# Window attention behind a depthwise convolution: attention blocks of one 8x8 patch and 32 channels, projection in quadrants, V transposed in the unit ring

## The chip, the core and the metric

The kernel runs on one core of one Trainium2 chip. The metric is the device time in microseconds. Below, PE is TensorE, DVE VectorE, ACT ScalarE, SP the engine that issues the loads and stores. All data is fp32.

## What is computed

x has the shape (4, 64, 128, 128). It is normalised in 32 groups of two channels and goes through a transposed channel attention, and x is added at the end:

```python
x = x + ref(gn(x))
qkv = einsum('bchw,oc->bohw', x, w_qkv) + b_qkv              # 192 channels
qkv = depthwise 3x3 convolution(qkv) + b_dw
# 8x8 windows, 4 heads of 16 channels; a window has 64 pixels
q, k, v = windows of qkv, each (windows, 4, 16, 64)
attn = softmax(einsum('nhcx,nhdx->nhcd', q, k) * temperature) # 16 x 16
out = einsum('nhcd,nhdx->nhcx', attn, v)
gate = gelu(einsum('nhcx,yx->nhcy', v, w_mlp) + b_mlp)        # exact gelu
out = einsum('bchw,oc->bohw', out * gate, w_proj) + b_proj
```

## The kernel before

Two images lie side by side in the 128 partitions (64 channels each), so there are two pairs of images. A pair is cut into 8 bands of 16 rows; a band of a pair is a chunk n, 16 in all. A chunk holds 64 windows (16 columns of windows, two window rows, two images). Work on chunk n + 1 up to q, k and v runs interleaved with the attention of chunk n.

The fore part of a chunk consists of units. 16 mix units (`mix_channels`, L674) put 10x10 patches through the 1x1 convolution: a unit is 4 matmuls, pixels on the output partitions. 6 depthwise units (`depthwise`, L709) multiply each channel's patch by a 103x64 matrix made from its taps: 32 matmuls a unit. One matmul of the source is two weight loads and two matmuls in the trace, a transpose one of each. Units share a ring of two PSUM buffers (`work`, two banks each in `unit_ps`). `units()` numbers all units in the order in which PE makes them; the parity of the number is the buffer. `take` makes PE wait until the unit two before it has been copied out, `wait_full` makes the copier wait for PE. ACT copies all mix units (z, L326) and most depthwise units (qkv, L326), DVE one a chunk (L417).

The attention of a chunk is four steps i of `BATCH` = 4 window groups, a = i % 4. A step is this chain:

- `score` (L747): per group, q times k with 64 pixels as contraction, for 64 columns of q (two windows of 32 channels) by 64 of k, into `score_ps`: 16 matmuls in 64x64 tiles. A 64x64 block also holds products between different windows and different heads, which are masked.
- DVE `scores_up`: adds the mask `other_head` (L511, 128x512), takes the maximum (L516), subtracts it (L518). ACT `exponent` (L341). DVE `divide`: sum (L532), reciprocal (L534), product (L536); `turn`: the 32x32 block transpose (L543) to `probs_t`.
- `turn_v` (L773): V of four groups is transposed on PE into `turn_ps`, one bank of `pair_ps`; ACT `v_up` (L347) copies it to `v_t`.
- `gates` (L763): V times w_mlp, 16 matmuls into `gate_ps`; DVE adds the bias (`gate_up`, L525), ACT does the gelu (L351), with table loads around it.
- `apply_probs` (L787): probabilities times V, 16 matmuls, into `pair_ps`; DVE `mix` multiplies by the gate (L503).
- `project` (L796): two matmuls of 128x128 by 256 columns, over a `proj` of 128x256 that is zero where a window half meets the other's channels, into `proj_ps`; DVE `residual` (L552) adds bias and x to `staged`, which SP stores by bands.

`pair_ps` holds three things in turn: `turn_ps` and the product of `apply_probs` use its first bank, `proj_ps` its second, so PE waits for `mixed_ready` of the step before ahead of `turn_v`, and for `out_ready` ahead of `apply_probs`.

The order of PE's work is written out by hand at the end of the PE block: score, some units (up to `cut[0]`), gates, project of the step before, turn_v, units up to `cut[1]`, gates, units up to `cut[2]`, apply_probs, the other units. Steps with a < 2 have 8 mix units each, a = 2 and a = 3 three depthwise units each. Gates are made in odd steps, two at once. ACT's and DVE's orders are written out in the same way; ACT is in step 0 and 1: two z copies, exp, v_t copy, six z copies; in step 2: v_t copy, exp, a qkv copy, gelus, a qkv copy; in step 3: exp, a qkv copy, v_t copy, gelu, qkv copy, gelu, qkv copy. The wait for both last depthwise units of a chunk stands before its first score (`qkv_of`).

## Time and profile before

| what | us |
|---|---|
| device time, three runs | 677.24, 678.43, 682.87 (median 678.43) |
| span of the profiled execution, first to last instruction | 680.0 |
| PE busy in it | 625.8 |
| DVE busy | 511.6 |
| ACT busy | 482.8 |

The profile gives no other time of its execution than the span; it is 1.6 us above the median of the runs. PE's busy time is made of modelled ends of matmuls that overlap, so starts are read rather than ends: how long a group takes is the distance from its first start to the first start of the next. PEld is the weight loads. "issue" is idle time for which the profile shows no releaser. Rows of the stretches view give busy time and, in brackets, the number of instructions that touch the stretch.

### The profile page before, as it was taken

The numbers are of one execution on the slowest core, as the hardware profiler recorded it, in microseconds if no ns is written. First come the engines' busy times: TensorE is split into PE (matmuls) and PEld (weight loads), VectorE is DVE, ScalarE is ACT, GpSimd is POOL, SyncE is SP. The second block draws the span as 40 slices with busy tenths as digits, with TensorE's granted clock in tenths as the row PEclk, the third lists the DMA queues.
The fourth block names the chain that finished last, engine by engine and source line by source line (L and its number), as shares of the span: only waits on it lengthen the run. The fifth ranks groups of instructions, "written<-read, shape, count | busy, mean of one in ns | idle before, by whom it ended". The sixth has DMA issues, their size and how long they took to land.

```text
span 680.0 us, 32438 instructions
## 1 busy us (share of the span) xinstructions
PE 625.8 (92%) x15044; PEld 549.1 (81%) x15044; DVE 511.6 (75%) x790; ACT 482.8 (71%) x631; POOL 0.3 (0%) x5
## 2 busy tenths in 40 slices
PE   3788799999999999999999999999999999999954
PEld 2687698888989898888989898888989798888843
DVE  4872688887888888786878676786868676876684
ACT  3652678787877778786877778786877778786722
...
PEclk9997899999999999999999999999999999999975
...
GB/s 363 263 217 72 33 50 166 110 86 208 33 232 49 234 59 149 66 102 93 8 191 5 195 4 142 60 94 106 29 173 4 198 3 152 44 50 80 4 82 44
DMA packets 29240, 72.28 MB, mean 106 GB/s; under 512 B 9801, under 2 KB 16329, under 8 KB 24233
## 3 DMA queue, kind: packets, MB, share of 16 engines
...
q8 instruction: 118, 1.93, 1.2%
...
q14 instruction: 16, 0.13, 0.1%
HBM read 53.44 MB, written 16.78 MB: 103 GB/s over the span
## 4 chain that ended last, share of the span: by engine, by line
PE 87%; ACT 5%; DVE 3%; issue 2%; DMA 1%; ACTq 0%; DVEq 0%
PE unit_ps L709 28%; PE unit_ps L674 26%; PE rest_ps L796 10%; PE rest_ps L787 6%; PE rest_ps L763 6%; PE rest_ps L747 6%; PE rest_ps L773 4%; ACT z L326 2%; DMA patches<-in_hot 1%; ACT dw L326 1%; PE rest_ps L643 1%; PE rest_ps L674 1%; PE unit_ps L636 0%; DVE scores L511 0%; DVE scores L536 0%
## 5 line engine op out<-in xcount | busy, mean ns | idle before, releaser
L326 ACT ACTIVATE z<-unit_ps 100x768 f32<-100x768 f32 x244 | 184.9, 808 | 60.1 <-PE unit_ps L674 60.1
L674 PE MATMUL unit_ps<-consts,patches 64*100 64x192 f32 x1984 | 195.0, 336 | 8.6 <-ACT z L326 6.6
L709 PE MATMUL unit_ps<-z,dw 103*64 103x64 f32 (+2 forms) x6144 | 194.3, 224 | 3.0 <-issue 1.7
L709 PEld LDWEIGHTS unit_ps<-z,dw 103*64 103x64 f32 (+2 forms) x6144 | 185.5, 139 | 10.7 <-issue 8.6
L674 PEld LDWEIGHTS unit_ps<-consts,patches 64*100 64x100 f32 x1984 | 153.6, 164 | 25.8 <-ACT z L326 11.2
L326 ACT ACTIVATE qkv<-unit_ps 128x1024 f32<-128x1024 f32 x78 | 79.1, 1014 | 31.5 <-PE unit_ps L709 31.4
L511 DVE TENSOR_TENSOR scores<-rest_ps,consts 128x512 f32<-128x512 f32 x64 | 44.1, 689 | 51.6 <-PE rest_ps L747 51.6
L503 DVE TENSOR_TENSOR gate<-rest_ps,gate 128x512 f32<-128x512 f32 x64 | 44.1, 689 | 47.5 <-PE rest_ps L787 44.6
L796 PE MATMUL rest_ps<-gate,consts 128*128 128x256 f32 x256 | 75.1, 417 | 1.1 <-DVE gate L503 1.0
L347 ACT ACTIVATE v_t<-rest_ps 128x512 f32<-128x512 f32 x64 | 38.2, 597 | 40.5 <-PE rest_ps L773 38.9
L341 ACT ACTIVATE scores<-scores 128x512 f32<-128x512 f32 x64 | 40.4, 631 | 33.2 <-DVE scores L518 31.6
L787 PE MATMUL rest_ps<-v_t,probs_t 64*64 64x64 f32 x2048 | 45.5, 228 | 10.5 <-DVE probs_t L543 10.1
L525 DVE TENSOR_TENSOR gate<-rest_ps,consts 128x512 f32<-128x512 f32 x64 | 44.0, 687 | 14.4 <-PE rest_ps L763 14.0
L796 PEld LDWEIGHTS rest_ps<-gate,consts 128*128 128x128 f32 x256 | 44.9, 195 | 11.9 <-issue 3.5
L747 PE MATMUL rest_ps<-qkv 64*64 64x64 f32 x2048 | 45.4, 227 | 9.0 <-issue 9.0
L787 PEld LDWEIGHTS rest_ps<-v_t,probs_t 64*64 64x64 f32 x2048 | 36.7, 137 | 20.9 <-issue 18.8
L747 PEld LDWEIGHTS rest_ps<-qkv 64*64 64x64 f32 x2048 | 37.9, 138 | 18.1 <-issue 18.1
L552 DVE SCALAR_TENSOR_TENSOR staged<-rest_ps,consts,staged 128x512 f32<-128x512 f32 x64 | 46.7, 729 | 7.5 <-PE rest_ps L796 7.5
L543 DVE STREAM_TRANSPOSE probs_t<-scores 128x512 f32<-128x512 f32 x64 | 45.5, 712 | 2.2
L763 PE MATMUL rest_ps<-consts,qkv 64*64 64x64 f32 x2048 | 45.6, 228 | 1.6 <-DVE scores L511 1.6
L763 PEld LDWEIGHTS rest_ps<-consts,qkv 64*64 64x64 f32 x2048 | 36.7, 138 | 12.3 <-issue 8.2
L518 DVE TENSOR_TENSOR scores<-scores,neg_max 128x512 f32<-128x512 f32 x64 | 44.3, 692 | 2.2
...
## 6 DMA issues: line engine op xcount, KB each, us to landing
...
```

Source lines behind the costliest of these rows:

```text
L326: return nc.scalar.activation(to, of, ACT.Copy)
L503: nc.vector.tensor_tensor(held, pair_ps[:, :, 0:BATCH * HW], held, ALU.mult).then_inc(mixed_ready, 1)
L511: nc.vector.tensor_tensor(scores[:].rearrange("p (h g) d -> p h g d", h=2), score_ps[:, :, 0:BATCH * C].rearrange("p h (g d) -> p h g d", ...
L518: nc.vector.tensor_tensor(scores[:], scores[:], neg_max[:].unsqueeze(2).to_broadcast([P, WIDE, C]), ALU.add).then_inc(shifted, 1)
L543: nc.vector.transpose(probs_t[:].rearrange("p w d -> p (w d)"), scores[:].rearrange("p w d -> p (w d)")).then_inc(probs_t_ready, 1)
L552: nc.vector.scalar_tensor_tensor(to, proj_ps.rearrange("p (r c) -> p r c", r=BAND), b_proj, to, op0=ALU.add, op1=ALU.add).then_inc(out_rea ...
L674: last = nc.tensor.matmul(to[0:NPATCH, t, b * QKV:(b + 1) * QKV], patches[image, b, g], w1[image], start=True, stop=True)
L709: last = nc.tensor.matmul(to[h * HW:(h + 1) * HW, m // 8, m % 8 * NW:(m % 8 + 1) * NW], dw[0:used, c, :], z[0:used, c, :], start=True, sto ...
L747: last = nc.tensor.matmul(score_ps[pair, h, g * C:(g + 1) * C], q[rows, pair], k[rows, pair], start=True, stop=True)
L763: last = nc.tensor.matmul(gate_ps[side(b, h), b, g * HW:(g + 1) * HW], windows(j, g)[rows, 2, b * C:(b + 1) * C], mlp[rows], start=True, s ...
L787: last = nc.tensor.matmul(pair_ps[side(b, h), b, g * HW:(g + 1) * HW], probs_t[rows, h * BATCH + g, :], v_t[rows, at], start=True, stop=True)
L796: last = nc.tensor.matmul(proj_ps[:, b * 4 * HW:(b + 1) * 4 * HW], proj[:, b * P:(b + 1) * P], gate[:, i % GATES, b].rearrange("p g (r c) ...
```

## The change

A block of the attention becomes one 8x8 patch of one image and 32 channels (two heads), in tiles of 32 columns. `score`, `gates` and `apply_probs` issue 32 matmuls each instead of 16. Scores, softmax and `probs_t` have 256 columns instead of 512 (`HALF` = 32 instead of `C` = 64 channels). `project` issues 4 matmuls, each of 64x64 weights by 256 columns, in the four quadrants, and its weights have no zeros. The result of `apply_probs` lies in the first halves of the two banks of `pair_ps`, that of `project` in the second halves. V is transposed into a buffer of the unit ring: ("turn", i) is a unit with a number of its own, so each step has one unit more, `turn_v` waits for its buffer instead of for `mixed_ready`, and `v_up` frees it. Constants loaded at the start are smaller by 160 columns.

```diff
@@ -64,7 +66,8 @@
     order = [("mean", 0), ("var", 0)]
     order += [("dw", 0, v) for v in range(3 * HALF // SPLIT)]
     for i in range(STEPS):
-        order += fillers(i)
+        fill, at = fillers(i), cuts(i)[0]
+        order += fill[:at] + [("turn", i)] + fill[at:]
     return {name: at for at, name in enumerate(order)}
 
 
@@ -84,6 +87,12 @@
     return fill
 
 
+def cuts(i):
+
+    a = i % BATCHES
+    return (2, 4, 6) if a < 2 else (0, 1, 3) if a == 2 else (1, 2, 3)
+
+
 def gates_in(i):
 
...
         T = sb("T", [P, BAND + 2, W + 2])
         patches = sb("patches", [P, 2, COLS, NPATCH])
         seen = sb("seen", [P, 2, STAT_ROWS, W])
-        scores = sb("scores", [P, WIDE, C])
-        probs_t = sb("probs_t", [P, WIDE, C])
+        scores = sb("scores", [P, WIDE, HALF])
+        probs_t = sb("probs_t", [P, WIDE, HALF])
         v_t = sb("v_t", [P, BATCH * P])
         gate = sb("gate", [P, GATES, 2, BATCH, HW])
...
@@ -131,7 +140,7 @@
         zeros = sb("zeros", [P, 2 * (BAND + 2)])
         norm = sb("norm", [P, PAIRS, 2])
 
-        sizes = (P, P, HW, 2 * P, QKV, C, HW, 1)
+        sizes = (P, P, HW, 2 * C, QKV, HALF, HW, 1)
         consts = sb("consts", [P, sum(sizes)])
         at = [sum(sizes[:n]) for n in range(len(sizes) + 1)]
         ident, group_mean, mlp, proj, w1, other_head, b_mlp, b_proj = (
@@ -148,9 +157,9 @@
         work = [unit_ps[:, 0:2], unit_ps[:, 2:4]]
         quarter = [half[:, 2 * m:2 * m + 2] for half in banks for m in range(2)]
         pair_ps = rest_ps[:, 0:2]
-        turn_ps, proj_ps = pair_ps[:, 0], pair_ps[:, 1]
-        score_ps = rest_ps[:, 2:4]
-        gate_ps = score_ps[:, :, BATCH * C:]
+        mix_ps, proj_ps = pair_ps[:, :, 0:BATCH * HW], pair_ps[:, :, BATCH * HW:]
+        gate_ps = rest_ps[:, 2:4, BATCH * HW:]
+        score_ps = rest_ps[:, 2:4, 0:BATCH * HALF]
 
         x_in = [sem(f"x_in{n}") for n in range(BANDS)]
...
@@ -234,7 +241,7 @@
 
             unit = ("dw", n, v)
             if n > 1:
-                engine.wait_ge(v_t_done, (n - 1) * BATCHES)
+                wait_full(engine, ("turn", (n - 1) * BATCHES - 1))
             wait_full(engine, unit)
             kind, at = kind_of(v)
             copy(qkv[:, n % 2, kind, :, at:at + SPLIT],
@@ -341,10 +348,11 @@
                 nc.scalar.activation(scores[:], scores[:], ACT.Exp).then_inc(exp_ready, 1)
 
             def v_up(i):
-                act.wait_ge(v_t_done, i + 1)
+                unit = ("turn", i)
                 if i:
                     act.wait_ge(mix_done, i)
-                nc.scalar.activation(v_t[:], turn_ps, ACT.Copy).then_inc(v_t_ready, 1)
+                wait_full(act, unit)
+                copy(v_t[:], work[buffer(unit)][:, 0]).then_inc(free[buffer(unit)], 1)
 
             def gelu(j):
...
                 held = gate[:, i % GATES].rearrange("p b g y -> p b (g y)")
-                nc.vector.tensor_tensor(held, pair_ps[:, :, 0:BATCH * HW], held, ALU.mult).then_inc(mixed_ready, 1)
+                nc.vector.tensor_tensor(held, mix_ps, held, ALU.mult).then_inc(mixed_ready, 1)
 
             def scores_up(i):
...
                 dve.wait_ge(scores_done, i + 1)
                 if i:
                     dve.wait_ge(probs_t_ready, i)
-                over = [P, 2, BATCH, C]
+                over = [P, 2, BATCH, HALF]
                 nc.vector.tensor_tensor(scores[:].rearrange("p (h g) d -> p h g d", h=2),
-                                        score_ps[:, :, 0:BATCH * C].rearrange("p h (g d) -> p h g d", d=C),
+                                        score_ps.rearrange("p h (g d) -> p h g d", d=HALF),
                                         other_head.unsqueeze(1).unsqueeze(1).to_broadcast(over),
                                         ALU.add).then_inc(masked, 1)
                 dve.wait_ge(masked, i + 1)
                 nc.vector.tensor_reduce(neg_max[:], scores[:], AX_X, ALU.max, negate=True).then_inc(max_ready, 1)
...
-                to = staged[:, n % 2, :, a * BATCH * WS:(a + 1) * BATCH * WS]
-                nc.vector.scalar_tensor_tensor(to, proj_ps.rearrange("p (r c) -> p r c", r=BAND),
+                to = staged[:, n % 2, :, a * BATCH * WS:(a + 1) * BATCH * WS].rearrange("p (b r) c -> p b r c", b=2)
+                nc.vector.scalar_tensor_tensor(to, proj_ps.rearrange("p b (r c) -> p b r c", r=WS),
                                                b_proj, to, op0=ALU.add, op1=ALU.add).then_inc(out_ready, 1)
 
...
@@ -730,8 +738,12 @@
                 at = 4 * (i % BATCHES * BATCH + g)
                 return qkv[:, i // BATCHES % 2, :, at:at + 4].rearrange("p k w c -> p k (w c)")
 
-            def side(b, h):
-                return slice((h ^ b) * HW, (h ^ b) * HW + HW)
+            def window(b, t):
+                return slice((2 * b + t) * HALF, (2 * b + t + 1) * HALF)
+
+            def place(b, t, h):
+                at = (2 * (t ^ b) + (h ^ b)) * HALF
+                return slice(at, at + HALF)
 
             def score(i):
 
@@ -740,12 +752,10 @@
                     pe.wait_ge(gate_biased, max(j for m in range(i) for j in gates_in(m)) + 1)
                 for g in range(BATCH):
                     q, k = windows(i, g)[:, 0], windows(i, g)[:, 1]
-                    for b in range(2):
-                        pair = slice(b * C, (b + 1) * C)
-                        for h in range(2):
-                            rows = slice(h * HW, (h + 1) * HW)
-                            last = nc.tensor.matmul(score_ps[pair, h, g * C:(g + 1) * C], q[rows, pair], k[rows, pair],
-                                                    start=True, stop=True)
+                    for b, t, h in product(range(2), repeat=3):
+                        rows = slice(h * HW, (h + 1) * HW)
+                        last = nc.tensor.matmul(score_ps[window(b, t), h, g * HALF:(g + 1) * HALF],
+                                                q[rows, window(b, t)], k[rows, window(b, t)], start=True, stop=True)
                 last.then_inc(scores_done, 1)
 
             def gates(j, i):
@@ -757,44 +767,42 @@
                     wait_free(pe, ("dw", j // BATCHES, 0))
                     wait_free(pe, ("dw", j // BATCHES, 1))
                 for g in range(BATCH):
-                    for b in range(2):
-                        for h in range(2):
-                            rows = slice(h * HW, (h + 1) * HW)
-                            last = nc.tensor.matmul(gate_ps[side(b, h), b, g * HW:(g + 1) * HW],
-                                                    windows(j, g)[rows, 2, b * C:(b + 1) * C], mlp[rows],
-                                                    start=True, stop=True)
+                    for b, t, h in product(range(2), repeat=3):
+                        rows = slice(h * HW, (h + 1) * HW)
+                        last = nc.tensor.matmul(gate_ps[place(b, t, h), b, g * HW:(g + 1) * HW],
+                                                windows(j, g)[rows, 2, window(b, t)], mlp[rows],
+                                                start=True, stop=True)
                 last.then_inc(gate_done, 1)
 
             def turn_v(i):
 
-                if i:
-                    pe.wait_ge(mixed_ready, i)
+                unit = ("turn", i)
+                to = take(unit)
                 for g in range(BATCH):
-                    last = nc.tensor.transpose(pair_ps[:, 0, g * P:(g + 1) * P], windows(i, g)[:, 2], ident)
-                last.then_inc(v_t_done, 1)
+                    last = nc.tensor.transpose(to[:, 0, g * P:(g + 1) * P], windows(i, g)[:, 2], ident)
+                last.then_inc(full[buffer(unit)], 1)
 
             def apply_probs(i):
 
-                pe.wait_ge(v_t_ready, i + 1)
+                wait_free(pe, ("turn", i))
                 pe.wait_ge(probs_t_ready, i + 1)
                 if i:
                     pe.wait_ge(out_ready, i)
                 for g in range(BATCH):
-                    for h in range(2):
+                    for h, b, t in product(range(2), repeat=3):
                         at = slice((2 * g + h) * HW, (2 * g + h + 1) * HW)
-                        for b in range(2):
-                            rows = slice(b * C, (b + 1) * C)
-                            last = nc.tensor.matmul(pair_ps[side(b, h), b, g * HW:(g + 1) * HW],
-                                                    probs_t[rows, h * BATCH + g, :], v_t[rows, at],
-                                                    start=True, stop=True)
+                        last = nc.tensor.matmul(mix_ps[place(b, t, h), b, g * HW:(g + 1) * HW],
+                                                probs_t[window(b, t), h * BATCH + g, :], v_t[window(b, t), at],
+                                                start=True, stop=True)
                 last.then_inc(mix_done, 1)
 
             def project(i):
 
                 pe.wait_ge(mixed_ready, i + 1)
-                for b in range(2):
-                    last = nc.tensor.matmul(proj_ps[:, b * 4 * HW:(b + 1) * 4 * HW], proj[:, b * P:(b + 1) * P],
-                                            gate[:, i % GATES, b].rearrange("p g (r c) -> p r g c", c=WS),
+                for b, t in product(range(2), repeat=2):
+                    rows = slice((t ^ b) * C, (t ^ b) * C + C)
+                    last = nc.tensor.matmul(proj_ps[t * C:(t + 1) * C, b], proj[rows, b * C:(b + 1) * C],
+                                            gate[rows, i % GATES, b].rearrange("p g (r c) -> p r g c", c=WS),
                                             start=True, stop=True)
                 last.then_inc(proj_done, 1)
 
@@ -815,7 +823,7 @@
             for i in range(STEPS):
                 units_now = fillers(i)
                 now = gates_in(i)
-                cut = (2, 4, 6) if i % BATCHES < 2 else (0, 1, 3) if i % BATCHES == 2 else (1, 2, 3)
+                cut = cuts(i)
                 if i % BATCHES == 0:
                     qkv_of(i // BATCHES)
...
     w_proj = np.asarray(L0_conv_w_proj)
-    proj = np.zeros((2, 2, HALF, 2, 2, C), f)
-    for b in range(2):
-        for h in range(2):
-            for t in range(2):
-                proj[h ^ b, t, :, b, t] = w_proj[:, h * HALF:(h + 1) * HALF].T
+    by_half = w_proj.T.reshape(2, HALF, C)
+    proj = np.stack([np.concatenate([by_half[b], by_half[1 - b]] * 2) for b in range(2)], 1)
     arrays = {
         "x": np.asarray(x),
```

PE in step 1 of a chunk (a = 1), from project to apply and the units behind it, before. `free0` and `free1` are the ring's buffers, `masked` and `gate_biased` DVE's passes:

```order
L796 MATMUL rest_ps<-gate,consts 128x256 [waits mixed_ready]
L796 MATMUL rest_ps<-gate,consts 128x256
L773 MATMUL rest_ps<-consts,qkv 128x128 [waits mixed_ready]
L773 MATMUL rest_ps<-consts,qkv 128x128 x3
L674 MATMUL unit_ps<-consts,patches 100x192 [waits free0]
L674 MATMUL unit_ps<-consts,patches 100x192 x3
L674 MATMUL unit_ps<-consts,patches 100x192 [waits free1]
L674 MATMUL unit_ps<-consts,patches 100x192 x3
L763 MATMUL rest_ps<-consts,qkv 64x64 [waits gate_biased,masked]
L763 MATMUL rest_ps<-consts,qkv 64x64 x15
L674 MATMUL unit_ps<-consts,patches 100x192 [waits free0]
L674 MATMUL unit_ps<-consts,patches 100x192 x3
L674 MATMUL unit_ps<-consts,patches 100x192 [waits free1]
L674 MATMUL unit_ps<-consts,patches 100x192 x3
```

and now:

```order
L804 MATMUL rest_ps<-gate,consts 64x256 [waits mixed_ready]
L804 MATMUL rest_ps<-gate,consts 64x256 x3
L782 MATMUL unit_ps<-consts,qkv 128x128 [waits free1]
L782 MATMUL unit_ps<-consts,qkv 128x128 x3
L682 MATMUL unit_ps<-consts,patches 100x192 [waits free0]
L682 MATMUL unit_ps<-consts,patches 100x192 x3
L682 MATMUL unit_ps<-consts,patches 100x192 [waits free1]
L682 MATMUL unit_ps<-consts,patches 100x192 x3
L772 MATMUL rest_ps<-consts,qkv 32x64 [waits gate_biased,masked]
L772 MATMUL rest_ps<-consts,qkv 32x64 x31
L682 MATMUL unit_ps<-consts,patches 100x192 [waits free0]
L682 MATMUL unit_ps<-consts,patches 100x192 x3
L682 MATMUL unit_ps<-consts,patches 100x192 [waits free1]
L682 MATMUL unit_ps<-consts,patches 100x192 x3
```

The transpose writes `unit_ps` and waits for a ring buffer, and the buffers of the units behind it alternate the other way round; project is 4 matmuls and gates 32.

PE from apply of step 2 through the first gates of step 3, before:

```order
L787 MATMUL rest_ps<-v_t,probs_t 64x64 [waits out_ready,probs_t_ready,v_t_ready]
L787 MATMUL rest_ps<-v_t,probs_t 64x64 x15
L747 MATMUL rest_ps<-qkv 64x64 [waits gate_biased,masked]
L747 MATMUL rest_ps<-qkv 64x64 x15
L709 MATMUL unit_ps<-z,dw 64x64 [waits free1]
L709 MATMUL unit_ps<-z,dw 64x64 x31
L763 MATMUL rest_ps<-consts,qkv 64x64 [waits free0,free1,gate_biased,masked]
L763 MATMUL rest_ps<-consts,qkv 64x64 x15
```

and now:

```order
L794 MATMUL rest_ps<-v_t,probs_t 32x64 [waits out_ready,probs_t_ready,free0]
L794 MATMUL rest_ps<-v_t,probs_t 32x64 x31
L757 MATMUL rest_ps<-qkv 32x32 [waits gate_biased,masked]
L757 MATMUL rest_ps<-qkv 32x32 x31
L717 MATMUL unit_ps<-z,dw 64x64 [waits free0]
L717 MATMUL unit_ps<-z,dw 64x64 x31
L772 MATMUL rest_ps<-consts,qkv 32x64 [waits free1,free0,gate_biased,masked]
L772 MATMUL rest_ps<-consts,qkv 32x64 x31
```

The order is the same; the matmuls of apply, score and gates are twice as many, those of the unit between them are not. In the same chunk, ACT's v_t copy reads `unit_ps` and waits for `full0` or `full1` instead of `v_t_done`.

## Rows read from the trace of the kernel before

**Rows 1.** The profile's page: busy shares, granted clock, instruction queue, chain.
```profile
PE 625.8 (92%) x15044; PEld 549.1 (81%) x15044; DVE 511.6 (75%) x790; ACT 482.8 (71%) x631; POOL 0.3 (0%) x5
...
PEclk9997899999999999999999999999999999999975
...
q8 instruction: 118, 1.93, 1.2%
...
PE 87%; ACT 5%; DVE 3%; issue 2%; DMA 1%; ACTq 0%; DVEq 0%
```

**Rows 2.** Stretches: length, busy PE, PEld, DVE, ACT, POOL; clock, DMA share, GB/s.
```profile
453.36:491.36 38.00, 37.14 (x928) 32.62 (x929) 28.52 (x44) 29.47 (x40) 0.00 (x0) 1.00 0.27 90
480.69:491.36 10.67, 10.06 (x341) 9.23 (x333) 8.49 (x14) 8.49 (x12) 0.00 (x0) 1.00 0.03 6
```

**Rows 3.** The chain that ended last, in that chunk: start us, us, what.
```profile
480.87 0.47 PE rest_ps L747 x32
...
490.75 0.61 issue
```

**Rows 4.** Timeline of PE: four first matmuls of a score, then step 0.
```profile
309.55 0.29 PE L747 MATMUL rest_ps<-qkv 64*64 64x64 f32 x4
...
453.36 0.69 PE L747 MATMUL rest_ps<-qkv 64*64 64x64 f32 x32 [0.60 <-issue]
453.98 1.55 PE L674 MATMUL unit_ps<-consts,patches 64*100 64x192 f32 x16
455.46 1.13 PE L796 MATMUL rest_ps<-gate,consts 128*128 128x256 f32 x4
456.43 0.60 PE L773 MATMUL rest_ps<-consts,qkv 128*128 128x128 f32 x4
```

**Rows 5.** Timeline of step 3 of the same chunk, PE and ACT.
```profile
481.27 2.08 PE L709 MATMUL unit_ps<-z,dw 103*64 103x64 f32 x64
...
483.28 0.69 PE L763 MATMUL rest_ps<-consts,qkv 64*64 64x64 f32 x32
483.71 0.63 ACT L341 ACTIVATE scores<-scores 128x512 f32<-128x512 f32 x1 [1.17 <-DVE scores L518]
...
484.25 1.01 ACT L326 ACTIVATE qkv<-unit_ps 128x1024 f32<-128x1024 f32 x1
```

**Rows 6.** Groups of instructions by line: busy us, mean ns, idle before them.
```profile
L511 DVE TENSOR_TENSOR scores<-rest_ps,consts 128x512 f32<-128x512 f32 x64 | 44.1, 689 | 51.6 <-PE rest_ps L747 51.6
...
L534 DVE RECIPROCAL inv_total<-total 128x8 f32<-128x8 f32 x64 | 13.0, 203 | 2.2
```

**Rows 7.** Stretch of the last four steps, columns as in rows 2.
```profile
643.73:676.60 32.87, 19.77 (x356) 15.55 (x356) 24.84 (x40) 10.01 (x15) 0.00 (x0) 0.70 0.23 58
```

**Rows 8.** Three places where PE stops: stretches, PE's timeline, instruction queue (55.5:56.8, 99.9:101).
```profile
51.96:58.11 6.15, 4.48 (x154) 4.34 (x149) 2.42 (x2) 1.03 (x1) 0.00 (x0) 1.00 0.57 174
98.70:102.31 3.61, 3.56 (x160) 3.41 (x153) 3.42 (x6) 2.14 (x4) 0.00 (x0) 1.00 0.28 77
249.92:253.49 3.57, 3.57 (x150) 3.44 (x148) 3.54 (x6) 3.02 (x5) 0.00 (x0) 1.00 0.17 37
...
58.12 0.39 PE L709 MATMUL unit_ps<-z,dw 106*64 106x64 f32 x6 [1.68 <-issue]
...
101.56 0.69 PE L763 MATMUL rest_ps<-consts,qkv 64*64 64x64 f32 x32
102.32 1.02 PE L796 MATMUL rest_ps<-gate,consts 128*128 128x256 f32 x4
...
633.27 2.45 PE L709 MATMUL unit_ps<-z,dw 106*64 106x64 f32 x64
...
q8 instruction: 1, 0.02, 5.7%
...
q8 instruction: 1, 0.02, 5.2%
```

**Rows 9.** Stretch after the first stop, columns as in rows 2.
```profile
59.60:73.20 13.60, 11.42 (x158) 9.84 (x152) 6.18 (x9) 4.52 (x6) 0.00 (x0) 0.50 0.00 1
```

13 lines of the change are left out of this document (6 added, 7 removed).

## The prediction

> **What bounds the kernel now.** I read the page's busy shares first: TensorE (PE) is busy 92% of the span, VectorE (DVE) 75%, ScalarE (ACT) 71% [rows 1]. The granted clock is full but for two places near the ends. The chain that ended last is 87% PE. Next the table of stretches for one chunk of four steps, 453.36 to 491.36 us: 38.00 us, PE busy 37.14 of it with 928 matmul instructions, ACT 29.5, DVE 28.5 [rows 2]. So PE sets the pace. The largest exception is before the next chunk's score: 0.6 us of "issue" [rows 3], at a place where the code waits for ACT's last qkv copy.
>
> The page counts 15044 matmuls and as many weight loads, and DMA queue 8 (kind instruction) brought 1.93 MB in 118 packets: 64 bytes an instruction, 16 KB a packet, so one packet is 256 PE instructions, or 128 load-and-matmul pairs [rows 1]. PE's program is streamed in. I come back to this, since the change makes that program longer.
>
> **The change, as PE's work.** One matmul of the source is two pairs in the trace (16 for 32).
>
> Score, gates and apply: 16 matmuls on 64x64 tiles become 32 on tiles of 32 columns, eight tiles side by side instead of four. Four tiles now do 32 pairs from one group's start to the next in 0.62 us [rows 4], of which some 0.15 us is the change of tile shape: without one, from apply to score, the chain has 0.47 [rows 3]. Eight tiles with the same 64 moving columns need the same eight rounds if they really run side by side, so 64 pairs in 0.62 us; score, with 32 columns, perhaps 0.02 less. The other bound is the densest issue that the rows show over a whole group, 32 pairs in those 0.47 us, or 14.6 ns a pair: by it 64 pairs take 0.94 + 0.15 = 1.09 us, 0.47 more in each of 12 groups, 5.6 us a chunk. I take 0.62, since four pairs are seen to start within 0.03 us [rows 4], so that the issue is not what spaces them.
>
> Project: 4 instructions of 256 columns now last 0.97 us [rows 4]. They become 8 in four quadrants, so two rounds of 0.22, a first weight load, and a change of shape that was not there (0.15): 0.60. The turn's first weight load then has no project to hide behind, 0.10. Net -0.27 a step; from below, if the quadrants ran one after the other, +0.9. The gates already run four such quadrants, with both row halves on one bank, in 0.62 us for 32 pairs, so I take -0.27. Apply to score, from step 2 to 3, gets a change of shape that it did not have, +0.15. PE alone: 4 x -0.27 - 0.08 + 0.15 = -1.0 us a chunk.
>
> **The ring.** The turn of V now takes a buffer of the unit ring, and the second mix after it waits for ACT's v_t copy (0.6 us). In step 0, counted from score's start, project starts at 2.06, the turn at 2.66, its copy at about 3.40, after exp, so the buffer is free at 4.0; that mix is due at 4.03. The mix after it keeps such wait for ACT as it has. In step 3 dw 4 needs the copy of dw 3, which ACT does after exp; before, exp began 3.0 us into the step [rows 4, 5]. Three DVE passes in front of it shrink by 0.25 each, so dw 3's copy ends near 3.9 and dw 4 is due at 4.5. I cost the ring at nothing; if the copies came late it is 0.3 to 0.6 in steps 0, 1 and 3, 1.5 a chunk.
>
> **DVE and ACT.** Seven DVE passes over 128x512 become 128x256: 0.69 to some 0.44 by the slope against the 128x8 reciprocal (0.20); exp goes from 0.63 to some 0.44, by the slope between 512 and the 1.01 of a 128x1024 copy [rows 6]. PE hides all of it in the chunks. It shows in the last four steps, which have no units to fill them: score, add, max, subtract, exp, sum, reciprocal, product, transpose, apply stand one behind the other, and DVE is the busiest engine there, 24.8 of 32.9 us [rows 7]. Seven times 0.25 is 1.75 us a step, 7 us; from both sides 3 (other waits come last) and 7; I take 6.
>
> **The instruction stream.** PE's pairs in a chunk go from 928 to 928 + 12 x 32 + 4 x 4 = 1328, so 10.4 packets in 37.0 us, one each 3.56 us. What does one cost? At 56.2 us PE stops for 1.9 us in the midst of a depthwise unit, where the code has no wait. A packet of queue 8 moves between 55.5 and 56.8, at 5.7% of 16 engines in 1.3 us, which is 1.19 us; PE goes on at 58.12, some 1.35 after its end. Two weaker stops look the same: L796 starts at 102.32, 0.76 after gates where 0.63 is usual, and 1.4 after the end of the packet that starts at 99.95 and takes 0.92; and in the unit at 633.27 64 pairs last 2.45 us where 2.08 is usual [rows 5, 8]. From counts of pairs: a packet is asked for when PE's queue enters the one before, some 18 pairs ahead of the array, so PE has some 146 pairs to run meanwhile. Before the stop at 102.3 these lasted 3.61 us; before the first one, with a load of T on the queues, 6.15. The densest such stretch that does not stop lasts 3.57 [rows 8]. So the stream's turnaround is about 3.5 us on quiet queues (1.0 to start, 1.1 to move, 1.35 to be used), and the kernel already touches it: the two weak stops lie where apply, score and a depthwise unit, 128 pairs in some 3.1 us, follow one another.
>
> After the change that seam has apply and score back to back, 128 pairs in 1.24 us. From that apply through step 3 to the next score: 588 pairs, 4.6 packets, that PE would do in 11.6 us (two applies and two scores 2.4, three depthwise units 6.0, two gates 1.2, project and turn 1.3, the wait for ACT 0.7). The three depthwise units of step 2 cover one packet, about four turnarounds remain, 4 x 3.5 = 14.0: +2.4 us. In step 1 gates, mix and apply are 128 pairs in 2.6 to 2.9: +0.3. Loads on the other queues stretch a turnaround as at 56 us (a T load is issued at each chunk's end); I put that at +1.0 a chunk. The waits for ACT go under these stops, -0.5. Sum +3.2; from both sides 0 (the chunks of now, which do not stop) and some 10, with four turnarounds of 6.15 instead of 3.5 there.
>
> The Trainium skill speaks against this term (Runtime: NRT & Kernel Launch, Instruction fetch mechanics): the fetch of 16 KB blocks is autonomous and hidden by the issue rate, and PE's instruction memory is given as 128 KiB. The trace agrees on the 16 KB; with that much in store (2048 instructions, by the page) the stop at 56.2 us would not be there. By the page the sum is rival A.
>
> **Sum.** Chunk: -1.0 + 3.2 = +2.2, times 15 = +33. Last four steps -6. The fill of the pipeline: 0. Span 680.0 + 27 = 707.0. The span of the profiled execution stands 1.6 above the median of the runs, 678.4, so 705 us.
>
> **Rivals.**
> A: the stream is hidden, as by the page, and PE's work counts alone: 678.4 - 15 x 1.0 - 6 = 657. For it: the chunk of 38.00 us has no such stop, PE being busy 37.14 of it [rows 2]. Against: the three stops, and 3.57 us as the densest stretch without one. If half of the stream's term comes (a second request under way, say), 680: no change.
> B: the tiles of 32 columns are not issued faster than 14.6 ns a pair. 5.6 us more PE work a chunk, which then hides most stops (1.0 left): -1.0 + 5.6 + 1.0, times 15, -6: 756. Against: four pairs start within 0.03 us [rows 4]. The Trainium skill (TensorE: Matmul & The Clock Gate, Wait — 56ns, not 53.3ns?) goes further: no less than about 25 ns between starts, however small the matmul. By it a group of 64 pairs would take 1.6 us; the rows have 14.6 ns, so it gets no chance.
> C: the stops pull the clock down. After the stop at 56.2 the granted clock is 0.50 from 59.6 to 73.2 [rows 9], at which PE's work takes about twice as long: some 5 us lost. With a stop that long in every other chunk, 7 x 5 on top: 742. It decides from stops of near 1.9 us; mine are 0.5 to 1.6, longer under a load.
>
> Chances: my forecast 0.50 (its own range 690 to 725), A 0.16, half of the stream's term 0.10, B 0.11, C 0.13. A measurement here tells about 1% from no change: faster by more 0.19, within 0.08, slower by more 0.73. The range takes A in and ends short of B: 655 to 750.
>
> **What would show it.** Right: queue 8 with about 168 packets and 2.75 MB; matmuls 21444; step 3 near 12 to 13 us instead of 10.67 and steps 0 to 2 shorter than or like before; PE idle that the waits put to "issue", at places in the midst of groups; score, gates and apply at 0.6 us where nothing stops them; project 0.60 to the turn's start; DVE's passes at 0.44. Wrong: chunks of 37 us without such gaps (A); groups of 1.1 us with PE busy throughout (B); a granted clock below 0.97 as a mean (C); waits for ACT's v_t copy before a mix, which would be the ring.

## The result and the profile after

| | us |
|---|---|
| before, median | 678.13 |
| after, median of four runs | 781.42 (777.75 to 785.61) |
| ratio, with 95% interval | 1.151 (1.146 to 1.157) |
| span of the profiled execution, after (before 680.0) | 783.8 |
| first score to the score of step 60 | 66.0 to 746.6 (before 66.7 to 643.7) |
| that score to the end | 37.2 (before 36.3) |

The change costs 103 us, where 27 were forecast. The profiled execution of after is the longest of its four runs (785.61), so what is read from it may be up to 4 us, or 0.3 a chunk, above the median. Practically all of it lies in the chunks: from the score of step 4 to that of step 60, 14 chunks, the mean chunk is 45.42 us instead of 38.15. Its four steps are 12.41, 11.30, 8.64 and 13.07 us (before 9.11, 9.95, 8.39 and 10.71).

The page of after, for [rows 1]:

```profile
PE 669.9 (85%) x21444; PEld 552.8 (71%) x21444; DVE 411.4 (52%) x790; ACT 475.0 (61%) x631; POOL 0.3 (0%) x5
...
PEclk9999999999997999989999999989989998999976
...
q8 instruction: 168, 2.75, 1.4%
...
PE 82%; issue 10%; ACT 5%; DVE 2%; DMA 1%; ACTq 0%; DVEq 0%
```

Counts are as forecast: 21444 matmuls, 168 packets of instructions, 2.75 MB. PE's share falls to 85% though its busy time rises, "issue" goes from 2% to 10% of the chain, and the clock's row has dips in the middle that [rows 1] do not have. DVE has lost 100 us of work, and nothing of that is seen in the time.

One chunk and its step 3 as stretches (columns as in [rows 2]):

```profile
426.48:474.10 47.62, 40.52 (x1332) 33.75 (x1329) 22.64 (x44) 28.74 (x40) 0.00 (x0) 0.96 0.23 76
461.62:474.10 12.48, 10.88 (x467) 9.54 (x461) 6.79 (x13) 8.17 (x12) 0.00 (x0) 1.00 0.09 22
```

PE stands still for 7.1 of 47.6 us; in [rows 2] it was 0.9 of 38.0. Its timeline in this chunk shows where:

```profile
427.17 1.55 PE L682 MATMUL unit_ps<-consts,patches 64*100 64x192 f32 x16
428.64 0.65 PE L804 MATMUL rest_ps<-gate,consts 64*64 64x256 f32 x5
432.88 0.65 PE L804 MATMUL rest_ps<-gate,consts 64*64 64x256 f32 x3 [3.58 <-issue]
...
442.92 0.79 PE L772 MATMUL rest_ps<-consts,qkv 64*32 64x64 f32 x56
445.63 0.32 PE L772 MATMUL rest_ps<-consts,qkv 64*32 64x64 f32 x8 [1.91 <-issue]
...
460.84 0.85 PE L794 MATMUL rest_ps<-v_t,probs_t 32*32 32x64 f32 x64
461.62 0.76 PE L757 MATMUL rest_ps<-qkv 64*32 64x32 f32 x64
462.31 1.50 PE L717 MATMUL unit_ps<-z,dw 103*64 103x64 f32 x44
464.29 0.80 PE L717 MATMUL unit_ps<-z,dw 103*64 103x64 f32 x20 [0.48 <-issue]
465.02 0.86 PE L772 MATMUL rest_ps<-consts,qkv 64*32 64x64 f32 x64
465.81 0.66 PE L804 MATMUL rest_ps<-gate,consts 64*64 64x256 f32 x8
466.40 0.66 PE L782 MATMUL unit_ps<-consts,qkv 128*128 128x128 f32 x4
466.99 2.13 PE L717 MATMUL unit_ps<-z,dw 103*64 103x64 f32 x64
```

PE stops within groups that have no wait inside: after 5 of project's 8 matmuls, after 56 of 64 in gates, after 44 of 64 in a depthwise unit. I counted PE's instructions against the packets of queue 8: a pause of more than 0.33 us between two starts, at the end of a packet to within two pairs, is called a stop below; shorter ones, as that in the unit at 633.27 of before [rows 8], are not counted. There are 59 in the 14 chunks, 76.2 us together, and PE goes on 1.2 to 1.6 us after the next packet has landed, every time. The longest have company on the queues. For 429 to 433.5 us (a T load of 1152 KB was issued at 424.9), the first line gives what the queues moved, in 40 slices:

```profile
GB/s 328 328 246 287 287 287 205 410 246 328 432 205 205 82 41 0 0 0 0 0 0 0 0 0 0 0 0 0 0 0 0 0 0 0 0 0 0 0 0 0
...
q1 hardware_dynamic: 108, 0.42, 33.3%
q8 instruction: 1, 0.02, 1.6%
```

The queues carry 200 to 430 GB/s until about 430.5; the packet of instructions starts at 430.22 and takes 1.14, and PE resumes at 432.88.

The groups themselves: project to turn 0.59 us (465.81 to 466.40) and turn to the next 0.59, where it was 0.97 and 0.53 [rows 4]; gates 0.79 (465.02 to 465.81), apply 0.78, score 0.69, where each was 0.62. One of DVE's passes over 256 columns, and ACT's exp, for [rows 6]:

```profile
L519 DVE TENSOR_TENSOR scores<-rest_ps,consts 128x256 f32<-128x256 f32 x64 | 27.2, 424 | 80.2 <-PE rest_ps L757 80.1
...
L348 ACT ACTIVATE scores<-scores 128x256 f32<-128x256 f32 x64 | 26.5, 414 | 29.4 <-DVE scores L526 29.4
```

And the end of the kernel, from the score of step 60, for [rows 7]:

```profile
749.64 0.66 PE L782 MATMUL unit_ps<-consts,qkv 128*128 128x128 f32 x4
752.10 1.17 PE L794 MATMUL rest_ps<-v_t,probs_t 32*32 32x64 f32 x64 [1.80 <-DVE probs_t L551]
753.20 0.84 PE L757 MATMUL rest_ps<-qkv 64*32 64x32 f32 x58
756.48 0.33 PE L757 MATMUL rest_ps<-qkv 64*32 64x32 f32 x6 [2.44 <-issue]
...
768.80 1.17 PE L794 MATMUL rest_ps<-v_t,probs_t 32*32 32x64 f32 x64 [2.73 <-DVE probs_t L551]
769.91 0.46 PE L757 MATMUL rest_ps<-qkv 64*32 64x32 f32 x31
772.25 0.49 PE L757 MATMUL rest_ps<-qkv 64*32 64x32 f32 x33 [1.88 <-issue]
```

DVE's shorter passes bring apply forward, and then the score behind it, on which DVE's next pass waits, stops in its midst.

### The profile page after: what moved, and what is told of

Read it like the earlier page. It is cut to its first block, busy times and chain, and to the rows that moved or that the text cites. A ratio compares the mean times of both kernels' runs of the same rounds, so it can differ in the third digit from the quotient of the medians.

```text
span 783.8 us, 45238 instructions
## 1 busy us (share of the span) xinstructions
PE 669.9 (85%) x21444; PEld 552.8 (71%) x21444; DVE 411.4 (52%) x790; ACT 475.0 (61%) x631; POOL 0.3 (0%) x5
## 3 DMA queue, kind: packets, MB, share of 16 engines
q8 instruction: 168, 2.75, 1.4%
## 4 chain that ended last, share of the span: by engine, by line
PE 82%; issue 10%; ACT 5%; DVE 2%; DMA 1%; ACTq 0%; DVEq 0%
PE unit_ps L717 25%; PE unit_ps L682 25%; PE rest_ps L772 7%; PE rest_ps L794 6%; PE rest_ps L757 6%; PE rest_ps L804 6%; PE unit_ps L782 5%; ACT z L333 2%; ACT dw L333 1%; DMA patches<-in_hot 1%; ACT qkv L333 1%; PE rest_ps L651 1%; PE rest_ps L682 1%; DVE staged L560 0%; PE unit_ps L644 0%
## 5 line engine op out<-in xcount | busy, mean ns | idle before, releaser
L333 ACT ACTIVATE v_t<-unit_ps 128x512 f32<-128x512 f32 x64 | 38.2, 598 | 79.1 <-PE unit_ps L782 78.6
L757 PE MATMUL rest_ps<-qkv 64*32 64x32 f32 x4096 | 52.0, 201 | 31.9 <-issue 28.3
L757 PEld LDWEIGHTS rest_ps<-qkv 64*32 64x32 f32 x4096 | 42.8, 107 | 45.0 <-issue 42.6
L794 PE MATMUL rest_ps<-v_t,probs_t 32*32 32x64 f32 x4096 | 59.4, 229 | 11.9 <-DVE probs_t L551 6.1
L772 PE MATMUL rest_ps<-consts,qkv 64*32 64x64 f32 x4096 | 58.4, 229 | 11.6 <-issue 8.8
L794 PEld LDWEIGHTS rest_ps<-v_t,probs_t 32*32 32x32 f32 x4096 | 46.5, 107 | 25.0 <-issue 21.0
L772 PEld LDWEIGHTS rest_ps<-consts,qkv 64*32 64x32 f32 x4096 | 46.2, 108 | 23.9 <-issue 20.6
L804 PE MATMUL rest_ps<-gate,consts 64*64 64x256 f32 x512 | 49.1, 439 | 7.0 <-issue 6.1
L782 PEld LDWEIGHTS unit_ps<-consts,qkv 128*128 128x128 f32 x256 | 29.6, 152 | 27.4 <-issue 24.2
L782 PE MATMUL unit_ps<-consts,qkv 128*128 128x128 f32 x256 | 46.1, 307 | 0.0
(55 smaller groups left out, 433.5 us busy)
```

Source lines behind the costliest of these rows:

```text
L333: return nc.scalar.activation(to, of, ACT.Copy)
L757: last = nc.tensor.matmul(score_ps[window(b, t), h, g * HALF:(g + 1) * HALF], q[rows, window(b, t)], k[rows, window(b, t)], start=True, st ...
L772: last = nc.tensor.matmul(gate_ps[place(b, t, h), b, g * HW:(g + 1) * HW], windows(j, g)[rows, 2, window(b, t)], mlp[rows], start=True, st ...
L782: last = nc.tensor.transpose(to[:, 0, g * P:(g + 1) * P], windows(i, g)[:, 2], ident)
L794: last = nc.tensor.matmul(mix_ps[place(b, t, h), b, g * HW:(g + 1) * HW], probs_t[window(b, t), h * BATCH + g, :], v_t[window(b, t), at], ...
L804: last = nc.tensor.matmul(proj_ps[t * C:(t + 1) * C, b], proj[rows, b * C:(b + 1) * C], gate[rows, i % GATES, b].rearrange("p g (r c) -> p ...
```

## The experiments

The theory after the result: the stops at packets' ends are nearly the whole loss, some made longer by loads, and the clock falls with them. The rivals: the 32-column tiles themselves, the ring, the quadrants. The measures of all kernels stand in one table. "Pairs" is what a chunk issues; chunk, stops and half clock are taken from the score of step 4 to that of step 60 of the profiled execution (stops a chunk, half clock in all).

| kernel | pairs | time, ratio (95%) | chunk | stops | half clock |
|---|---|---|---|---|---|
| before | 928 | 678.1 | 38.15 | 0 | 0 |
| after | 1328 | 781.4, 1.151 | 45.42 | 5.44 | 54.6 |
| a1 after, one row | 1328 | 750.8, 1.107 (1.102 to 1.112) | 42.91 | 3.77 | 17.1 |
| a2 before, one row | 928 | 676.4, 0.997 (0.995 to 0.999) | 38.14 | 0 | 0 |
| a3 before, more pairs | 1312 | 794.6 and 811.1 | 46.30 | 2.62 | 17.1 |
| a4 before, turn in ring | 928 | 686.0, 1.012 (1.009 to 1.014) | 38.58 | 0.03 | 0 |
| b1 after, score later | 1328 | 786.0, 1.160 (1.156 to 1.163) | 45.27 | 4.09 | 37.5 |
| b2 after, pieces | 1328 | 797.6, 1.177 (1.174 to 1.180) | 45.49 | 4.60 | 47.8 |
| b3 before, 32 channels | 1184 | 720.7, 1.063 (1.061 to 1.066) | 41.33 | 2.25 | 3.4 |
| c1 after, dw joined | 1040 | 693.3, 1.023 (1.020 to 1.025) | 39.50 | 1.21 | 6.8 |
| c2 before, dw joined | 640 | 663.2, 0.978 (0.976 to 0.981) | 37.31 | 0.03 | 0 |

### Fewer bytes on the other queues (a1, a2)

```diff
-                rows = slice(band_of(n) * BAND, (band_of(n) + 1) * BAND)
-                sp.dma_start(bands[n // BANDS, :, rows, :], staged[:, n % 2]).then_inc(stored[n % 2], 16)
+                rows = slice(band_of(n) * BAND, band_of(n) * BAND + 1)
+                sp.dma_start(bands[n // BANDS, :, rows, :], staged[:, n % 2, 0:1]).then_inc(stored[n % 2], 16)
```

The loads of T, staged and seen are cut in the same way.

> The changed kernel; from chunk 2 on the loads of T, staged and seen and the stores move one row instead of 18, 16, 4 and 16, so most of the input is not loaded and most of the output not stored. PE's program is the same, 168 packets. Stream theory (PE stops at the end of each 16 KB packet until the next has come, and the loads on the other queues lengthen the turnaround): still some four stops a chunk, none over 1.8 us where the changed kernel has 4.4, no stretch at half clock between 110 and 700 us; 725 us (700 to 745). Rival (the 32-column tiles or their PSUM banks stop PE, whatever the queues do): 775 to 785 with stops of up to 4 us.

> The kernel before with the same loads and stores cut to one row. Stream theory: nearly no packet is late there, so 673 to 679 us: only the stop of 1.9 us at 56 us is shorter, or the stretch at half clock behind it. A theory in which the loads slow PE by themselves: under 665 us.

After gains 31 us, before 2. So the loads matter, and only together with the longer program: the stops of step 0 fall from 2.14 to 0.84 us a chunk, those of step 1 from 0.79 to 0.10, and those above 2 us from 31.9 us in all to 2.6. The changed kernel's half clock falls from 54.6 to 17.1 us, where I had expected none, and the longest stop from 4.4 to 2.6, where I had expected 1.8. But step 3, where few bytes run, keeps its 2.3 (2.75 now), and 3.77 us a chunk stay. My 725 was too low: the loads are about a third of the loss, not half. The profiled execution of after is its longest and that of a1 the shorter of two; by the medians, 31 us apart, a chunk differs by some 2.1 us (an estimate) instead of 45.42 - 42.91 = 2.5.

### More instructions, the tiles of before (a3), and the ring alone (a4)

a3 adds to each matmul of score, gates and apply one of a single column (here score):

```diff
+                            few = slice(b * C, b * C + 40)
+                            nc.tensor.matmul(score_ps[few, h, g * C:g * C + 1], q[rows, few],
+                                             k[rows, b * C:b * C + 1], start=True, stop=True)
```

> The kernel before; ahead of each of the 16 matmuls of score, gates and apply one more of 40 weight columns and one moving column, whose result the next overwrites. 1312 pairs a chunk instead of 928 (the change: 1328), all tiles 64x64, no other edit. PE's work alone: eight more rounds of some 35 ns a group, 0.3 x 12 = 3.4 us a chunk, less the waits that it hides: 720 us. Stream theory: on top some four stops a chunk at the ends of packets, with half clock after the long ones: 770 us (745 to 790). The rival (the change's stops come from its tiles): 715 to 725 without stops.

```profile
q8 instruction: 166, 2.72, 1.4%
...
436.27 0.48 PE L807 MATMUL rest_ps<-gate,consts 128*128 128x256 f32 x1
440.77 1.39 PE L807 MATMUL rest_ps<-gate,consts 128*128 128x256 f32 x3 [4.02 <-issue]
```

These are the page's line of queue 8 and PE's timeline. With before's tiles, project and ring, the same stops are there, also behind a T load, 39 of them, again ending 1.2 to 1.6 us after a packet. So the stops need neither the narrow tiles nor the quadrants; the number of instructions brings them. The time says less, and it is above the 745 to 790 that I had written down: the added matmuls cost PE about 5 us a chunk beside the stops (46.30 - 38.15 - 2.62), more than the 3.4 that I had assumed, and that is also why it has fewer stops than after. Its two runs lie 2% apart and the profiled one is the longer, so I take from it that the stops are there, not their exact size.

a4 is the diff's `units`, `v_up`, `turn_v` and the waits on `free` alone, in the kernel before.

> Only the third part of the change: V's transpose is a unit of the ring, all else as before. 928 pairs a chunk. Turn still follows a project of the same tile shape. If the ring costs nothing: 678 us (676 to 680). If PE waits for ACT's copies of v_t or of dw 3, which is late here since DVE's passes are as long as before: dw 4 waits 0.5 to 1.0 us in step 3, 0.3 in step 0, so 686 to 695, with rows of PE unit_ps behind ACT qkv or v_t in the waits.

Eight us, 0.43 a chunk: the ring isn't free. The waits of PE's weight loads for the ring's copiers, of a4, then of before, then of c1 (below), which has the ring with DVE's short passes:

```profile
PEld unit_ps L680 <- ACT z L331: 12.2, 29, 3.0
PEld unit_ps L680 <- ACT v_t L331: 7.7, 30, 0.8
```

```profile
PEld unit_ps L674 <- ACT z L326: 11.2, 15, 3.0
```

```profile
PEld unit_ps L682 <- ACT v_t L333: 7.1, 30, 0.2
```

The waits for z are nearly as long in before. Those for the v_t copy are new, and with 7.7 us they are of the size of the loss.

### Another order, and transfers in pieces (b1, b2)

```diff
-                if i % BATCHES == 0:
+                if i == 0:
+                    qkv_of(0)
+                fill(units_now[:cut[0]])
+                if i and i % BATCHES == 0:
                     qkv_of(i // BATCHES)
-                if i == 0:
-                    fill(units_now[:cut[0]])
                 score(i)
-                if i:
-                    fill(units_now[:cut[0]])
```

> The kernel after; in each step score now stands behind the units of the first cut, so that apply and score are no longer neighbours from step 2 to 3 and from step 0 to 1 (the number of PE instructions is the same). Theory, the stops come where PE gets through a packet of 128 pairs faster than the stream turns around (about 3.5 us): the densest stretch is gone, step 3 falls from 13.07 to about 12.2 us, the stops from 5.4 to 4.0 us a chunk, the time from 781 to 760 (750 to 770). Rival, what counts is the number of instructions alone (each packet beyond some number costs a stop wherever it lies): 781 within 5, step 3 at 13. If score later makes apply late, the waits show it by a wait for DVE's probs_t ahead of apply, and the time goes up.

The stops do shrink by what I said, 5.44 to 4.09 us a chunk, step 3's from 2.32 to 1.68. The time does not: 786, where 750 to 770 was expected, and which taken alone is what the rival said. The waits of b1:

```profile
PE rest_ps L772 <- DVE scores L519: 16.3, 31, 0.6
...
PE unit_ps L682 <- ACT z L333: 8.7, 23, 3.3
```

Gates come right behind score now and wait for DVE's mask pass (their PSUM banks are shared), about 1 us a chunk (16.3 in all, 1.1 in after), and ACT's exp comes later, its z copies with it (8.7, in after 2.8). The chunk is as long as in after, 45.27 against 45.42. What the stops gave, 1.35 us, and the clock, these waits took, as far as they can be added up; the rest of the time lies in the first steps and the last.

b2 issues each transfer as four, each behind the one before it:

```diff
-                sp.dma_start(T[:, to:to + hi - lo, 1:1 + W], halves[n // BANDS, :, lo:hi, :]).then_inc(t_in, 16)
+                for m in range(PIECED):
+                    if m:
+                        sp.wait_ge(t_in, ((n - 1) * PIECED + m) * 16)
+                    a, z_ = (hi - lo) * m // PIECED, (hi - lo) * (m + 1) // PIECED
+                    sp.dma_start(T[:, to + a:to + z_, 1:1 + W],
+                                 halves[n // BANDS, :, lo + a:lo + z_, :]).then_inc(t_in, 16)
```

> The kernel after; the loads of T, those of staged and the stores go in 4 pieces, each issued when the one before has landed, with the same bytes. With these transfers cut to one row each the time was 751. Theory, a packet of the instruction queue waits behind what already stands on the 16 DMA engines: with a quarter of it in flight at a time the stops above 2 us nearly vanish, 755 to 765, granted clock 0.96 or more. Rival, the bytes as such take the engines' time, in whatever pieces: 775 to 790, with stops of 3 us and more as before. If a piece comes too late for DVE (T ahead of the patches), a wait for it shows and the time is above 790.

A miss, and a poor test. SP waits for each piece, so later transfers start late: the first score comes at 79.3 instead of 66.0, and the chain of b2 now holds DMA:

```profile
PE 65%; DMA 19%; issue 8%; DVE 4%; ACT 3%; SPq 1%; ACTq 0%; DVEq 0%
```

In the chunks the stops fall only to 4.60 us, with one of 3.5 left. Those above 2 us do shrink, from 31.9 us in all to 10.9, and those of step 0 from 2.14 to 1.0 us a chunk. Whether smaller bursts without such waits would help is not answered by it.

### The dose of instructions (b3, c1, c2)

b3 gives the kernel before only the 32-channel score, softmax and apply:

```diff
+                    for b, t, h in product(range(2), repeat=3):
+                        rows, win = slice(h * HW, (h + 1) * HW), slice((2 * b + t) * HALF, (2 * b + t + 1) * HALF)
+                        last = nc.tensor.matmul(score_ps[win, h, g * HALF:(g + 1) * HALF], q[rows, win], k[rows, win],
+                                                start=True, stop=True)
```

> The kernel before; only score, softmax and apply go by 32 channels (256 columns of scores, 32-column tiles), while gates, project and the turn of V stay as before: 1184 pairs a chunk, between 928 and 1328. Groups of 64 pairs at 0.70 (score) and 0.79 us (apply) instead of 0.62 cost +1.0 a chunk, the change of shape at project is not there. Theory (turnaround of about 3.5 us, worse where loads run): the stretch from apply of step 2 through step 3 is still too dense, about 2 us of stops a chunk, chunk 41, time 720 (705 to 740). Rival 1 (only the mean rate counts, 9.25 packets in 39 us are 4.2 us each): no stops, 690 to 697. Rival 2 (8-column tiles side by side bring stops by themselves, however many instructions): as after, 770 or more.

720.7 with 2.25 us of stops a chunk: the theory's number, and neither rival's. On the mean a packet has 4.5 us here, and the stops come all the same, most of them in the dense step 3, which takes 12.09 us.

c1 and c2 take instructions out of the depthwise units, which both kernels have, at the same number of columns:

```diff
-                for m in range(SPLIT):
+                for m in range(0, SPLIT, 4):
                     for h in range(2):
                         c = kind * C + h * HALF + at + m
-                        last = nc.tensor.matmul(to[h * HW:(h + 1) * HW, m // 8, m % 8 * NW:(m % 8 + 1) * NW],
-                                                dw[0:used, c, :], z[0:used, c, :], start=True, stop=True)
+                        last = nc.tensor.matmul(to[h * HW:(h + 1) * HW, m // 8, m % 8 * NW:(m % 8 + 4) * NW],
+                                                dw[0:used, c, :], z[0:used, c:c + 4, :].rearrange("p c w -> p (c w)"),
+                                                start=True, stop=True)
```

> The kernel after; a depthwise unit issues 8 matmuls of 256 columns instead of 32 of 64: four neighbouring channels go with the matrix of the first of them, so three channels in four get another channel's taps. The number of columns, and so PE's time for the unit, stays; a chunk has 1040 pairs instead of 1328, 8.1 packets of which none comes quickly. This leaves of the change only its work on PE and the ring. Theory (the stops, and the clock that follows them, are all that the change costs): no stops, clock at before's 0.97, chunk 38.0 to 39.0 us, time 675 to 693, most likely 685: groups of 64 pairs +1.6, project -1.3, ring +0.4 a chunk. The prediction's own sum of PE's work was -1.0 a chunk, which would be 657. Rival (tiles of 32 columns or the quadrants cost something beside the stream): 700 or more, without stops at the packets' ends.

> The kernel before with the same edit of the depthwise units (8 matmuls of 256 columns instead of 32 of 64, three channels in four with another channel's taps): the control for the other one. 640 pairs a chunk. If a unit's time is its columns, the chunk stays at 38.1 and the time at 675 to 680 (the stops at the start, of 1.7 us, gone: up to -3). If the wider matmuls are slower or faster, this shows by how much.

c2's chunk is 0.84 us shorter than before's (a unit takes 1.88 instead of 2.01 us), which I had not expected, so that much is the edit's own. After's chunk falls by 5.92: 5.1 of the 7.27 us that the change costs go away with 288 pairs that the change has not touched. Not all stops do: I had expected none, and 1.21 us a chunk are left, most of them in step 1, so the time is at the upper edge of what was expected, 693. A chunk without a stop of c1, and one of c2, as stretches:

```profile
424.80:462.79 37.99, 37.39 (x1040) 26.86 (x1041) 22.23 (x44) 28.86 (x40) 0.00 (x0) 1.00 0.28 91
```

```profile
403.58:440.75 37.17, 36.31 (x640) 27.62 (x641) 28.43 (x44) 29.42 (x40) 0.00 (x0) 1.00 0.28 92
```

37.99 against 37.17: without stops the change still costs 0.8 us a chunk, in work of PE and in the ring, so even then it wins nothing in the chunks. The rival of c1, 700 or more without stops, falls too.

### The last four steps (b4, c3, d1, d2, d3)

b3's last four steps took 31.7 us, without a stop, against 36.3 of before, so DVE's passes are worth something there. b4 uses b3's edit in these steps alone:

```diff
+def narrow(i):
+
+    return i // BATCHES == CHUNKS - 1
```

> The kernel before; score, softmax and apply by 32 channels only in the last four steps, which have no units of another chunk to cover DVE and where few PE instructions are issued; the chunks are word for word as before. Theory (the prediction's term for the end: seven DVE passes a step at 0.42 to 0.44 us instead of 0.69, exp 0.2 less, all on the path): -5 us, 673 (671 to 675), ratio 0.990 to 0.995. Rival (the end did not get shorter in the kernel after, 37.1 us against 36.3, because other waits come last or the clock falls to half whatever DVE does): 677 to 680, ratio 0.998 to 1.002.

675.29 against 677.74, ratio 0.9966 (0.9944 to 0.9989): faster, by half of the 5 us expected. c3 leaves the very last step wide.

> The kernel before; score, softmax and apply by 32 channels only in steps 60, 61 and 62, not in the very last one. With all four, the time was 675.3 and the last score stopped for 2.6 us at a packet's end. Theory: the stop comes from the 128 pairs of apply and score that run through in 1.5 us ahead of it; with 32 pairs fewer there the packet's end falls elsewhere or is covered by DVE's passes: 673 (671 to 675), though the last step's DVE passes are 1.7 us longer. Rival (the stop only moves): 675 to 677.

677.03, ratio 0.9986 (0.9960 to 1.0012): not told from before. The stop is shorter, 1.4 us of idle time instead of 2.6, but still at the same pair, and the time is the upper end of the rival's, not the theory's. The last score, where it stops, and the apply of the step before it, of b4, then of c3:

```profile
657.68 0.84 PE L805 MATMUL rest_ps<-v_t,probs_t 32*32 32x64 f32 x64 [2.67 <-DVE probs_t L556]
658.45 0.32 PE L758 MATMUL rest_ps<-qkv 64*32 64x32 f32 x23
661.37 0.70 PE L758 MATMUL rest_ps<-qkv 64*32 64x32 f32 x41 [2.60 <-issue]
```

```profile
659.84 1.17 PE L805 MATMUL rest_ps<-v_t,probs_t 32*32 32x64 f32 x64 [2.67 <-DVE probs_t L556]
660.94 0.91 PE L764 MATMUL rest_ps<-qkv 64*64 64x64 f32 x23
663.27 0.58 PE L764 MATMUL rest_ps<-qkv 64*64 64x64 f32 x9 [1.42 <-issue]
```

PE resumes 3.69 and 3.43 us after apply's first matmul. In after it was 4.38 and 3.45 (752.10 to 756.48, 768.80 to 772.25). In b4 PE had entered the packet at 653.15 already, but the next one did not start to move before 658.62, 0.94 after apply was let go. In c3 it starts 0.95 after. This is the 3.5 us of my turnaround, counted from the end of a wait: as if the request for a packet stood behind apply's wait in PE's queue. If so, moving the packets' ends must move or remove the stop. d1 and d2 do that, with more and shorter idle products in the fill:

```diff
-            idle_products(24)
+            shorter_products(36)
```

> The kernel with 32 channels in the last four steps, and 24 pairs more in the fill of the pipeline (36 idle products of 128 columns instead of 24 of 192, the same columns), which moves each packet's end 24 pairs back in the program, nothing else. The packet's end that stopped the last score for 2.6 us (at 23 to 24 of its 64 pairs) then falls at its first pair, 64 behind apply's wait instead of 88. Theory (the request for a packet stands behind apply's wait when that wait comes early in the packet): the stop goes, end of the kernel 1.5 to 2.5 us shorter, 673 (671 to 675), ratio 0.991 to 0.995. Rival (the stores on the queues delay the packet, which they do wherever its end lies): the stop stays above 1 us, 675 to 677.

> The same, with 96 pairs more in the fill (72 idle products of 64 columns): the packet's end falls 32 pairs later than at first, at pair 56 of the last score, 120 behind apply's wait. Theory: the packet is asked for only once apply is released, PE resumes 3.4 to 3.7 us after apply's start and so stops for about 2.2 us, at pair 56. Time 674 to 677. Rival (the stores): a stop of another length, not tied to apply's start.

The same place, of d1, then of d2:

```profile
662.12 1.17 PE L810 MATMUL rest_ps<-v_t,probs_t 32*32 32x64 f32 x64 [2.67 <-DVE probs_t L556]
663.22 0.89 PE L763 MATMUL rest_ps<-qkv 64*32 64x32 f32 x64
664.07 2.07 PE L824 MATMUL rest_ps<-gate,consts 128*128 128x256 f32 x4
```

```profile
682.72 0.84 PE L810 MATMUL rest_ps<-v_t,probs_t 32*32 32x64 f32 x64 [2.67 <-DVE probs_t L556]
683.50 0.74 PE L763 MATMUL rest_ps<-qkv 64*32 64x32 f32 x55
686.28 0.34 PE L763 MATMUL rest_ps<-qkv 64*32 64x32 f32 x9 [2.04 <-issue]
```

In d1 the stop is gone, and the next packet moves at 659.03, well before apply at 662.12. In d2 the stop has moved to pair 55, the next packet moves at 683.84, 1.12 after apply was let go, and PE resumes 3.56 us after apply: the pair, the length and the interval that were written down. The rival with the stores falls for this stop. d1's time is nevertheless 677.8, ratio 0.9988 (0.9975 to 1.0000), and not the 671 to 675 expected, since another packet's end now lies in the gates of step 61 and stops PE for 1.7 us: the end takes 34.1 us, where it takes 34.2 in b4. d2's time, 701.5, comes for the most part from elsewhere, see the last section.

> The kernel before with the same 24 pairs more in the fill: the control. Its chunks do not stop and its last steps neither, so 676 to 680 (ratio 0.997 to 1.002); where a chunk now stops, the count of packets' ends in dense stretches was luck.

681.14, ratio 1.0031 (1.0018 to 1.0045), a bit above the range: two weak stops appear in the 14 chunks (1.1 us in all), where before had none. Part of before's quietness is where its packets end.

b4 is the one complete version that beats both kernels, by 0.3%. With the packets' ends moved by 24 pairs its edit is worth 3.3 us (d1's 677.8 against d3's 681.1), with them as they were 2.5; the two are not told apart. So its gain does not hang on where the ends fall, but the time of either kernel does, by a few us.

## Why the prediction was off

The direction was right, and so was the mechanism, stops at the ends of packets of instructions; the time (705) and the range (to 750) were not. What failed is the sum of a chunk: its terms for the loads, for the stops without them and for PE's work were too small, and the ring and the clock stood in it at nothing. Term by term, a chunk:

**Instruction stream, the named places.** For the seam and step 3 I had 2.4; step 3's stops are 2.32 and step 2's 0.20. For step 1 I had 0.3; it is 0.79 with the loads and 0.10 without. So the turnaround, read from three stops of before, gave the size of these steps where few bytes run. The sentence that failed is the next one: "Loads on the other queues stretch a turnaround as at 56 us [...]; I put that at +1.0 a chunk." Step 0, where the T load runs, has 2.14 us of stops, and I had not looked for a packet's end there. Measured, the loads are worth 2.5 (45.42 - 42.91, before's chunk staying at 38.14; some 2.1 by the medians), partly as longer stops and partly through the clock. With the loads cut to one row the stops are still 3.77 instead of my 2.7, of which 0.84 lie in step 0, for which I had no term.

**The clock.** Rival C was priced as something that happens instead of my forecast; it came on top. 54.6 us of the 14 chunks run at a granted 0.50, the level of 1.2 GHz, most of it within a few us of stops; half of that is lost at most, 1.95 us a chunk. In a1 it is 17.1 us, at most 0.6 a chunk. That stops cause it is argued from such neighbourhood and from the table (no stops, no half clock), not shown by a run of its own. The size of a single case says little: the stop near 58 us, from which rival C took its price, is followed in before by 13.6 us at 0.50 [rows 9]; in b4, where PE does the same up to there, PE is idle for 2.08 us instead of 1.68, and 3.4 us at 0.50 follow; in d1 it is idle for 2.75, and the clock stays full until 78.0.

**PE's work.** I had -1.0; c1 and c2 show +0.8 with the ring in it. Project was right (1.18 us with the turn instead of 1.50, so -1.3 for four steps, where I had -1.1). "I take 0.62" for the groups of 64 pairs was wrong: 0.69, 0.79 and 0.78 make +1.6. The bounds of 0.62 and 1.09 held it, and the reason for taking the lower one (four pairs starting within 0.03 us) spoke of four tiles, not of eight. Rival B, which took the upper one, is as wrong.

**The ring.** "I cost the ring at nothing" was wrong by 0.4 a chunk in a4, where DVE's passes are still long. With the short ones, in c1, the new waits for v_t are about as long (7.1 against 7.7 us), so I take the same cost there.

**The last four steps.** -6 was forecast and 0.9 was lost. DVE's passes were right at 0.42, and b3 shows what they are worth with no stop in the way, 4.6 us; the four stops of after there come to 7.9 us. The forecast asked only where PE is dense over a long stretch. It did not ask what happens to a packet's request while PE waits, on which b4, d1 and d2 bear.

**Sum.** Of the 5.1 us missing in a chunk, 1.8 are PE's work and the ring, 1.5 the loads, 1.1 the stops without loads, 0.6 the clock without loads. PE's work with the ring, which needed no stop at all, is the largest of them. 14 times 5.1 is 71, with some 7 for the end 78, and 1 less in the fill and the first chunk; the miss is 76 to 77. (Two of the recorded rivals' times don't follow from their own terms by 1 or 2 us: C's seven times 5 on top of 705 is 740, half of the stream's term 681. Nothing rests on it.)

Rival A is out: the Trainium skill's statement (Runtime: NRT & Kernel Launch, Instruction fetch mechanics) that the fetch is hidden by the issue rate does not hold here: with 1040 pairs in a chunk of 39.5 us 1.21 us of stops are left, and with 928 in 38.15 there is none in the chunks, but one of 1.9 us in the fill. Its 16 KB do hold: 168 packets, 2.75 MB. Each stop counted here lies at the end of a packet of 256 instructions and ends about 1.4 us behind the landing of the next; by the page's figure of 128 KiB, eight such packets, PE would have had enough in store to go on.
